# Prepared weights, edge blocks and the middle kernel row reordered in a two-layer style-conditioned attention and expert kernel

## The reference

```
x = x + attn0(cond(x, style));   x = x + ffn0(cond(x, style))
x = x + attn1(cond(x, style));   x = x + ffn1(cond(x, style))

cond: four layers (same, upsample, same, downsample), 3 taps,
      weight = SCALE * w * s;  weight *= rsqrt(sum(weight**2) + EPS);  out = conv(x, weight) + b
attn0: q, k, v = x @ Wqkv.T (32 query heads, 8 key/value heads of 128), rotary, causal softmax, @ Wo.T
attn1: the same with low-rank query and key/value projections;  ffn0, ffn1: a base product plus gated low-rank experts
```

## Time and profile before

| what | value |
|---|---|
| time, median of 3 runs | 964.35 us (964.32 to 966.01) |
| profiled execution, its own time | 964.44 us |
| its span | 962.6 us |
| TensorE busy | 940.2 us |
| VectorE / GpSimd / ScalarE busy | 544.4 / 479.5 / 237.6 us |
| mean granted TensorE clock | 0.998 of full |
| the 40 slices of the span | TensorE at 9 tenths or more in all but the first and the last |

### The profile page before, as it was taken

The page is one execution under the profiler, slowest core; times in us unless marked ns, Lnnn a source line. Parts: engine busy times, 40 slices in busy tenths (PEclk is TensorE's granted clock), DMA queues, the critical chain, the costliest instruction groups (busy, mean ns, idle before and its releaser), DMA issues.

```text
span 962.6 us, 16038 instructions
## 1 busy us (share of the span) xinstructions
PE 940.2 (98%) x6786; PEld 704.8 (73%) x6786; DVE 544.4 (57%) x930; ACT 237.6 (25%) x461; POOL 479.5 (50%) x442
## 2 busy tenths in 40 slices
PE   7999999999999999999999999999999999999997
PEld 3338887877888778887788778955968777546854
DVE  7866747657376473764836853462436979403332
ACT  5802122210211202112021130011034676610010
POOL 7945538497374873748827561410304756421300
PEclk9999999999999999999999999999999999999999
DMA  5693101211012110121101584097480000091002
GB/s 143 164 249 106 59 1 44 78 44 56 2 45 77 44 55 1 45 77 44 56 1 45 143 177 130 3 200 151 177 322 8 3 2 3 1 193 48 3 1 87
DMA packets 36303, 74.30 MB, mean 77 GB/s; under 512 B 13508, under 2 KB 22276, under 8 KB 33156
## 3 DMA queue, kind: packets, MB, share of 16 engines
q1 hardware_dynamic: 35896, 72.89, 27.0%
q10 hardware_dynamic: 336, 0.39, 0.1%
HBM read 66.26 MB, written 7.01 MB: 76 GB/s over the span
## 4 chain that ended last, share of the span: by engine, by line
PE 78%; DVE 9%; POOL 8%; issue 2%; ACT 1%; DMA 1%; POOLq 0%; DVEq 0%; SPq 0%
PE ps L1176 15%; PE ps L1244 15%; PE ps L1037 8%; PE ps L1321 5%; PE ps L1532 5%; PE ps L1190 5%; POOL w_lo L2470 3%; DVE arena L2127 3%; PE ps L1463 2%; PE ps L982 2%; PE ps L1465 2%; PE ps L1464 2%; PE ps L1221 1%; PE ps L1001 1%; DVE arena L2124 1%
## 5 line engine op out<-in xcount | busy, mean ns | idle before, releaser
L2599 POOL TENSOR_TENSOR arena<-arena 128x512 f32<-128x512 f32 x80 | 103.6, 1295 | 123.5 <-DVE arena L2127 123.3
L1176 PE MATMUL ps<-xt_hi,w_hi 128*128 128x512 f32 x320 | 128.5, 402 | 4.8 <-DVE arena L2127 2.1
L1176 PE MATMUL ps<-xt_lo,w_hi 128*128 128x512 f32 x320 | 126.0, 394 | 0.0
L1176 PE MATMUL ps<-xt_hi,w_lo 128*128 128x512 f32 x320 | 125.6, 392 | 0.0
L2127 DVE TENSOR_TENSOR arena<-ps,rope 64x512 f32<-64x512 f32 x160 | 110.2, 688 | 2.2
L2145 DVE TENSOR_TENSOR fresh<-ps,fresh 128x512 f32<-128x512 f32 x56 | 38.7, 691 | 119.7 <-PE ps L1244 119.6
L1244 PE MATMUL ps<-h_hi,wo_lo 128*128 128x512 f32 x224 | 82.1, 395 | 1.6 <-POOL wo_lo L2606 1.6
L1244 PE MATMUL ps<-h_hi,wo_hi 128*128 128x512 f32 x224 | 82.8, 400 | 0.0
L1244 PE MATMUL ps<-h_lo,wo_hi 128*128 128x512 f32 x224 | 81.9, 396 | 0.0
L1719 ACT ACTIVATE h_hi<-ps 128x512 fp32r<-128x512 f32 x64 | 33.1, 605 | 185.9 <-PE ps L1221 185.9
L1176 PEld LDWEIGHTS ps<-xt_hi,w_hi 128*128 128x128 f32 x320 | 60.3, 188 | 23.5 <-DVE arena L2127 4.7
(11 more groups left out here) (354 smaller groups left out, 1936.2 us busy)
## 6 DMA issues: line engine op xcount, KB each, us to landing
acts<-in_w_o_dram SPq DMA_DIRECT2D x8, 1024.0 KB, 5.0
arena<-in_a_wo_dram SPq DMA_DIRECT2D x6, 1024.0 KB, 7.8
arena<-kernel_rows SPq DMA_DIRECT2D x11, 512.0 KB, 12.1
acts<-in_w_qkv_dram SPq DMA_DIRECT2D x3, 1792.0 KB, 7.1
acts<-in_w_qkv_dram SPq DMA_DIRECT2D x4, 1280.0 KB, 6.6
w_l<-kernel_rows SPq DMA_DIRECT2D x10, 512.0 KB, 11.6
arena<-level_rows SPq DMA_DIRECT2D x3, 1024.0 KB, 20.9
stream<-in_x_dram SPq DMA_DIRECT2D x4, 512.0 KB, 6.6
```

The source lines that it names most:

```text
L1176: last = pe.matmul(ps[:, bank, :], w[:, r, cols], x, start=(r == 0 and n == 0), stop=(r == R - 1 and n == 2))
L2599: pool.tensor_tensor(qk[:, chunk, half * HALF:(half + 1) * HALF], rot[:, k % 2, 0, :], rot[:, k % 2, 1, :], ALU.add).then_inc(s_rope, 1)
```

## The change

- `kernel_first`: the four products of the middle row go to four column groups (partitions 0 to 127), none accumulated; VectorE copies the upper 64 partitions out of PSUM, adds the lower 64 to them, and then scales.
- `apply(0, g)` waits for tiles by bank for the first three groups, not for all 52 tiles at the first.
- `level_step(1)` moves between the halves of `kernel_second(2)`; on VectorE `level_step(0)` comes behind two tiles of net 2, and `first_scales` ahead of `turn_taps` of nets 2 and 3.
- Token groups: GpSimd splits part 0 after group 0 and parts 1, 2, 3 after groups 4, 5, 6.
- Round 1's weights: ScalarE's `round_qkv(1)` comes ahead of the evictions of the values of round 0, and for odd i doesn't wait for the values.
- Softmax of round 0: maxima and shift come right behind the pull and the mask, sum and turn at the same k as in other rounds.
- `edge_blocks`: both layers of a round at k == 7.

```diff
             def kernel_second(net, middle_step=None):
...
                     pe.matmul(d2[0:64], adjoint(net, ADJ_D2C1, 2), c1, **ADD).then_inc(s_cmp, 1)
+                    if h == 0 and middle_step is not None:
+                        level_step(middle_step)
...
                 for chunk, first in enumerate((ADJ_E2A, ADJ_E2B)):
                     for h in range(2):
-                        last = pe.matmul(o[h * C:(h + 1) * C], adjoint(net, first, 1), kern_d[:, chunk, columns(h)],
-                                         start=(chunk == 0), stop=(chunk == 1), skip_group_check=True)
+                        at = (2 * chunk + h) * C
+                        last = pe.matmul(o[at:at + C], adjoint(net, first, 1), kern_d[:, chunk, columns(h)],
+                                         start=True, stop=True)
...
                         pe.wait_ge(s_kern[net], 16 * 13)
-                        if net == 0:
-                            pe.wait_ge(s_cev, NCMP * NET)
...
                     if net == 0:
+                        if g < 3:
+                            pe.wait_ge(s_cev, NCMP * NET - 5 + g)
                         apply(net, g)
...
             kernel_third(2)
-            level_step(1)
-            kernel_second(2)
+            kernel_second(2, middle_step=1)
...
                     act.wait_ge(s_qkv, 10 * i)
-                    act.wait_ge(s_vt, 4 * ((i - 1) // 2) + 4)
+                    if i % 2 == 0:
+                        act.wait_ge(s_vt, 4 * ((i - 1) // 2) + 4)
...
+                round_qkv(1)
                 values(0, range(4))
-                round_qkv(1)
...
-                        bank = bank[0:2 * C]
                         dst = kern_mid[net % 2].rearrange("p (b o) -> p b o", o=C)
                         scale = mid_in[:, net, :].unsqueeze(2).broadcast_to([2 * C, HB, C])
+                        ch.link(dve.tensor_copy(dst, bank[2 * C:4 * C]))
+                        ch.link(dve.tensor_tensor(dst, bank[0:2 * C], dst, ALU.add))
+                        bank = dst
...
+            first_scales(slice(1, NET))
             turn_taps(slice(2, NET))
-            first_scales(slice(1, NET))
...
+            scaled_tiles(2, range(2))
             level_step(0)
-            scaled_tiles(2, range(4))
+            scaled_tiles(2, range(2, 4))
...
                 soft_pull(0, 0, probs)
+                soft_max(0, 0, probs, stat)
                 for i in range(NKV - 2):
                     for k in range(6):
                         rotate(i + 1, k)
-                        if i == 0 and k == 0:
-                            soft_max(0, 0, probs, stat)
-                        if k == (1 if i else 2):
+                        if k == 1:
                             soft_sum(i, 0, probs, stat)
-                        if k == (3 if i else 4):
+                        if k == 3:
                             soft_dense(i)
...
-                    if net == 0 and g < R:
+                    if net == 0 and g in (0, 4, 5, 6):
                         if g == 0:
                             pool.wait_ge(s_est[2], 64)
-                        split_qkv(0, (g,))
+                        split_qkv(0, (g - 3 if g else 0,))
...
                 soft_mask(0, 0, probs)
+                soft_shift(0, 0, probs, stat)
                 for i in range(NKV):
                     for k in range(10):
                         if i + 1 < NKV:
                             rope_add(i + 1, k)
-                        if i == 0 and k == 0:
-                            soft_shift(0, 0, probs, stat)
-                        if i < NKV - 1 and k == (1 if i else 2):
+                        if i < NKV - 1 and k == 1:
                             soft_scale(i, 0, probs, stat)
...
                         if i < 6 and k == 7:
-                            edge_blocks(1 + i // 2, 2 * (i % 2))
+                            for layer in range(2):
+                                edge_blocks(1 + i // 2, 2 * (i % 2) + layer)
                     if i + 2 < NKV:
                         split_qkv(i + 2)
-                    if i < 6:
-                        edge_blocks(1 + i // 2, 2 * (i % 2) + 1)
```

More of the change, by code:

```diff
@@ L983, in kernel_third, with kernel_second @@
                                   start=True, stop=True).then_inc(s_cmp, 1)
-            def kernel_second(net):
+            def kernel_second(net, middle_step=None):
                 pe.wait_ge(s_adj, 2 + 3 * min(net, 2))
```

## The result

The changed kernel takes 952.84 us, median of 4 runs (952.67 to 953.85), against 964.4 of the kernel before beside it (4 runs, 964.32 to 966.01): a ratio of 0.9881, 95% interval 0.9866 to 0.9896. The forecast was 951.5, so 1.3 of the 12.9 that it summed did not come. The profiled execution is the slowest of the four (953.85, span 952.1; the other spans are 950.9 to 951.1).

The account below looks back on a forecast made before the run. The prediction took TensorE, busy for 98% of the span, as the bound nearly everywhere. Part A 1.6, Part B 5.1 and Part C 6.2 sum to 12.9 us: 964.44 - 12.9 = 951.5, range 949.8 to 956.5.

Parts of the forecast that it names:

- Part B: Second round: earlier weight rounding and the softmax of round 0 bring back 5.1 us, bounds 4.0 and 5.1.
- Part C: Edge layers at k == 7: three rounds with late masks get back 2.07 us each, 6.2 in all, bounds 3.6 and 6.2.
- The first rival: Edge layers give only the named idle, 3.6 us instead of 6.2, so 954.1; chance 0.13.
- the fourth: GpSimd bounds attention: edge layers hold up rotary sums of tiles 8 and 9; slower, about 967; chance 0.02.
- Part A: Kernel rows to the first attention tile: faster middle rows and new token order save 1.6 us, bounds 0 and 2.9.
- the kernel rows: Net 0 gives back its saving and 0.2 more, nets 1 to 3 give 0.8 each; `apply(0, 0)` starts 2.2 us earlier.
- The second term: Tokens: the patch stops deciding, the splits do; the first tile waits 1.0 us for part 3, ending at 103.4.
- The third: The wait for part 3 brings the clock to 1.2 GHz, 1.6 us back, so 953.1; chance 0.12.
- The fifth: Banks or the patch's DMAs still gate as before: Part A at 0, others whole, 953.1; chance 0.12.
- The second: The softmax piece stays and Part A gives nothing because part 3 comes late: 954.2; chance 0.08.
- the softmax piece: Second round: the softmax of round 0, begun right behind the pull, is on time for `pv`; 1.1 us back.
- its own three lower bounds: Lowest savings of the three parts: Part A 0, Part B 4.0, Part C 3.6 us, giving 956.8.

Follow-up runs that it names:

- kernel 3: The kernel before with Part C alone, both edge layers of a round at k == 7: 958.17 us, ratio 0.9931.
- Kernel 10: As kernel 8 (earlier biases), but with the splits of parts 1 to 3 back behind token groups 1 to 3: 951.58 us, ratio 0.9868.
- Kernel 7: The changed kernel with the old middle row, two column groups and one multiplication out of the bank: 953.82 us, ratio 0.9891.
- 11: As kernel 8, with the first net's middle row back to two column groups and one multiplication: 949.57 us, ratio 0.9846.
- kernel 6: The changed kernel with the first round's splits of parts 1 to 3 back behind token groups 1 to 3: 952.41 us, ratio 0.9875.
- kernel 5: The changed kernel with parts 1, 2, 3 split behind token groups 2, 3, 4 instead of 4, 5, 6: 951.75 us, ratio 0.9866.
- kernel 4: The kernel before with Part A alone (the changed kernel with Part B and Part C put back): 964.94 us, ratio 1.0003.
- The second set: The changed kernel run again with no edit: 955.19 us, ratio 0.9904.
- kernel 8: As kernel 5, with VectorE's bias instructions moved from behind tile 7 of the second net's kernel rows to behind tile 5: 950.39 us, ratio 0.9855.

## Why the prediction was right, and where it was not

**Part B, right.** Forecast 5.1, measured 4.98 in the stretch and 4.8 to 5.1 in time. The steps hold singly: rounding 130.34 to 132.97 (forecast 130.2 to 132.8), split until 139.86 (139.7), first value bank evicted at 133.03 (132.9), no clock below 1.00 at 147, and the pieces 4.0 and 1.0.

**Part C, right.** Forecast 6.2, measured 6.17 in the trace and 6.3 in time. In the changed kernel TensorE's lead over the kernel before grows from 4.91 at the third round (197.65 against 202.56) to 11.08 at the eighth (503.09 against 514.17): 6.17 over the three disturbed rounds, as in kernel 3. The first rival, by which only the named waits come back, falls. So does the fourth: GpSimd still idles at least 5.12 before a ninth rotary sum.

**Part A, wrong: 1.6 forecast, nothing measured.** The time was inside the range because A's lower bound was nothing. Two terms were mis-sized, and the table separates them.

The first is the kernel rows, forecast at 2.2, measured 1.20 (67.92 to 66.72). Net 0 went as written: `kernel_second(1)` at 33.85, forecast 33.7, with a wait of 1.30 in which TensorE's saving ended. Then the forecast took 0.8 off for each net. The last stretch, from `kernel_second(3)` to the application, gave 0.84, the one before it 0.51 (15.94 for 16.45, with the moved level step, 0.33, now inside it). From `kernel_second(1)` to `kernel_second(2)` it gave 0.14 (15.43 for 15.57) although that level step had left it: there stands the wait of 0.93 at 49.28. The step that failed is "In nets 1 to 3 VectorE has several us of gaps and catches up". In the changed kernel the gaps lie before tiles 4 and 6 of net 1 (0.36 and 1.56); behind tile 7 follow the four bias instructions, four evictions, the middle row's three instructions and the two tiles that `kernel_second(2)` wants, without a gap. Kernel 10, with the biases in a gap, takes 1.07 off that stretch. I counted the gaps of the whole net where only one behind the last piled-up work would have counted.

A second part of that wait was not foreseen. VectorE's bias instructions themselves grew. In the kernel before:

```profile
40.54 0.22 DVE L1956 TENSOR_SCALAR mid_scale<-arena 128x128 f32<-128x128 f32 x1
40.67 1.09 DVE L1958 TENSOR_TENSOR mid_bias<-arena,cbias 128x128 f32<-128x128 f32 x3
```

In the changed kernel:

```profile
40.97 0.56 DVE L1959 TENSOR_SCALAR mid_scale<-arena 128x128 f32<-128x128 f32 x1
41.45 1.98 DVE L1961 TENSOR_TENSOR mid_bias<-arena,cbias 128x128 f32<-128x128 f32 x3
```

From start to end they take 1.22 and 2.46, so 1.24 are added, beside some 1.4 for the middle row's two new instructions. Kernel 7, with the old row, has 1.21. At their old length the wait of 0.93 would, by this estimate, not have arisen. Why they grew no run shows; GpSimd runs at both times.

What gave the 1.2 was not the middle row either. With the old middle row, kernel 7 has the same sum (66.77). Its net 0 takes 17.80, no longer 18.75 (another 0.19 are in net 2, where the level step moved), and what is left of the change in net 0 is the order of `first_scales`. GpSimd's half rows start sooner, 15.65 after the first `kernel_third` in kernel 7 against 16.59 in the kernel before, and the start of net 1 follows them. In the changed kernel they start at 26.44, against 27.54 and a forecast of 26.65. By the table's stretches the changed kernel is 0.84 shorter than kernel 7 in net 3, 0.70 longer in net 1, where the wait of 1.30 is, and 0.31 longer in net 2, where that of 0.93 is. In net 0 it is 0.22 shorter, but TensorE waits there for GpSimd, whose half rows came 0.23 later in kernel 7 counted from the first `kernel_third`; the changed kernel run again has 17.79 there, and kernels 10 and 11, with the new and the old row, have 17.56 and 17.54. So this is not the column groups' gain, and without it they lost 0.2. With both waits removed, by the old row in net 0 and the earlier biases (11), the sum is 64.70.

The second term is the token order. From the application to the values the forecast was 0.3 to 0.6 more than before, measured 1.20 more (52.34 against 51.14). The patch did come forward and stopped deciding, as forecast: 100.46 is where TensorE's own groups end. It stopped only just: its first transfer is issued at 89.78, where the forecast had 88, and its last 2.50 ahead of the tile, against 2.41 and 2.46 where TensorE waited for it. And the patch had been only 0.9 late with the old order (kernel 6). In exchange part 3 came at 104.5, forecast 102.6. Of that 1.9, 1.0 is the application's later start, 0.4 the first split (done at 97.02, forecast 95.6), because group 4 has to come first and GpSimd idled for it, and 0.5 are the two pairs of group and split behind it, at 3.74 where the forecast had 3.4 and 3.6. The bound named for this case, "part 3 at 104.5", was the outcome. Splits two groups sooner have no wait and still let the patch through (50.34 in kernel 5): the order was right in kind and two groups too late.

The two terms meet by accident: -1.20 and +1.20, so "nothing" in kernel 4 is a gain and a loss of one size, not an edit without effect.

**The other rivals.** The third fell: no clock below 1.00 behind a wait of 1.78. The fifth was right on the sum (953.1) and wrong on the cause. It had the banks or the patch gate as before; the banks and patch did not gate, a split did. The second was half right: A gave nothing because part 3 came late, as it says, but the softmax piece came back. The Trainium skill's warning (TensorEngine Tiling (Array Packing), Performance Considerations), that evacuation of PSUM may become the bottleneck, was weighed as true of net 0 alone. Here the trace agrees with it for the middle rows of nets 0 and 1, with 1.30 and 0.93 of wait behind them against 0.84 saved in each, and the forecast gave it too little. Two things add to it here: VectorE's own work for the row grew from 0.67 to some 2.1, because the sum of the two chunks moved to it, and the bias instructions grew as told above.

**What is left of the gap.** 951.5 + 1.6 = 953.1 against 952.84 and 955.19: the three parts measured (0, 4.98, 6.2) explain the first set to 0.4. The second set is not explained. The two profiled executions agree better: the lead of 11.08 at the eighth round, less the wait of 0.56 for the late load, is the 10.5 by which the spans differ (962.6 and 952.1). So nothing later ate any of it, as forecast.

**Sums of the prediction that do not come out.** The two idle times 2.1 and 1.6 make 3.7, not 3.6. The range ends at 956.5, below the 956.8 of its own three lower bounds. And the fourth rival's 10.5 us a layer counts 8.29 of idle time in all six rounds, where three of them have 10.5 to 10.9; with these the loss would need a layer of about 11.6. None of this bears on the outcome.

## What to carry to other kernels

A faster TensorE step is worth what the engine behind it can pass on at that very place. Look for the last full gap in that engine's queue before the result is wanted, not for gaps in general. When a queue's order is changed to let something urgent through, work out when the work that was put off is wanted: here one position later was worth 0.9 to 1.1 (kernel 5 against 6, kernel 8 against 10), and three positions later cost 1.15. A late start of a group, taken as a difference of starts against an undisturbed round, was a better measure of a wait's price than the idle time that names it (2.07 a round against some 1.2).

## What the runs showed of the hardware

The first `kernel_third` took 3.67 us in two profiled executions and 5.45 to 6.47 in the other twelve. TensorE's stretches in the kernel before and in part C alone, with one and the same front (us, busy, granted clock, DMA share, GB/s):

```profile
13.00:15.00 2.00, 2.00 (x3) 1.00 1.21 280
15.00:17.00 2.00, 2.00 (x4) 1.00 0.17 30
```
```profile
13.00:15.00 2.00, 1.76 (x5) 1.00 1.14 281
15.00:17.00 2.00, 0.39 (x1) 1.00 0.29 59
```

Both say 1.00, yet the eight matmuls end at 17.3 in the one and 14.8 in the other. The same eight matmuls take 3.70 in nets 2 and 3, so it is the twelve executions that ran slowly. The view does not show a lower grant at the start, so the cause stays open. Of the 2.65 that part C alone is shorter there, TensorE spends 1.85 waiting for ScalarE's weights (L1601) in front of `kernel_second`, which is why the second line shows it at work for only 0.39; the whole effect is 1.0 to 1.2 us in net 0's stretch (18.75 against 17.52 with the old front, 17.56 against 16.58 with the new one). It is also enough to make the first executions of two kernels differ by as much as a small edit gives.

The 96 value matmuls of round 0 took 10.78 to 10.80 us from first start to last in twelve executions and 11.19 in two (part C alone and kernel 5), with no gap between them. Nothing here tells why.

GpSimd's token sum over 512 columns took 1.64 to 1.75 beside VectorE's work here, while the rotary sum of the same shape took 1.30; no run isolates the cause. VectorE's four bias instructions took 1.2 in the kernel before, 2.5 in the changed kernel and 1.7 in kernel 8, where they stand a few us earlier, so a move changes durations too. Eight 32-column passes in four column groups took 1.07, in two groups 1.91.
